# A threshold search over router scores: comparing against base plus step, with the base kept by an accumulator

## What is computed

```python
x = x + xattn(layernorm(x), ctx, ctx, Wq, bq, Wk, bk, Wv, bv)   # softmax(Q K^T / 16) V
# ffn on xt = layernorm(x), 4096 x 256; E = 8 experts, k = 4096 * 2 / 8 = 1024
S = sigmoid(xt @ Wg).T            # 8 x 4096
G, I = top_k(S, k)                # each expert takes its 1024 best rows
ex = xt[I]                        # 8 x 1024 x 256
hid = gelu(ex @ W1 + b1)          # 8 x 1024 x 1024
out = (hid @ W2 + b2) * G
x = x + zeros.at[I].add(out)
```

## Time and profile before

| what | value |
|---|---|
| median of 3 runs | 569.58 us |
| profiled execution | 573.77 us |
| its span | 571.9 us |
| PE busy | 498.6 us (87%) |
| DVE busy | 349.2 us (61%) |
| ACT busy | 303.8 us (53%) |
| POOL busy | 297.3 us (52%) |
| mean granted clock of PE | 0.923 of full speed |

### The profile page before, as it was taken

The page is one execution under the profiler, slowest core; times in us unless marked ns, Lnnn a source line. Parts: engine busy times, 40 slices in busy tenths (PEclk is TensorE's granted clock), DMA queues, the critical chain, the costliest instruction groups (busy, mean ns, idle before and its releaser), DMA issues.

```text
span 571.9 us, 10360 instructions
## 1 busy us (share of the span) xinstructions
PE 498.6 (87%) x3667; PEld 354.5 (62%) x3667; DVE 349.2 (61%) x759; ACT 303.8 (53%) x544; POOL 297.3 (52%) x431
## 2 busy tenths in 40 slices
PE   4599898898633339999999999999999999999995
PEld 4378587676531124586487487487487487487484
DVE  4468888887678863754754753753753853842721
ACT  3556555444723304925934934943943943953931
POOL 2435988797460041673564564474465365366045
PEclk9989899898855556999999999999999999999998
DMA  8952444554351012494484385385385376274024
GB/s 212 309 198 76 107 112 107 146 130 120 93 142 51 0 44 70 131 176 66 132 166 75 119 159 92 111 151 107 108 145 116 101 144 124 85 157 56 0 29 47
DMA packets 92343, 64.57 MB, mean 113 GB/s; under 512 B 53076, under 2 KB 88216, under 8 KB 92312
## 3 DMA queue, kind: packets, MB, share of 16 engines
q1 hardware_dynamic: 79664, 46.82, 30.9%
q0 software_dynamic: 12288, 17.05, 18.3%
q10 hardware_dynamic: 360, 0.30, 0.2%
HBM read 36.22 MB, written 16.91 MB: 93 GB/s over the span
## 4 chain that ended last, share of the span: by engine, by line
PE 59%; POOL 12%; DVE 7%; issue 7%; SPq 6%; DMA 6%; ACT 3%; POOLq 0%; DVEq 0%; ACTq 0%
PE bank L980 54%; SPq L260 6%; POOL xn L366 3%; DMA rows_d<-xrow 3%; PE bank L1185 3%; POOL xrow L359 2%; POOL out L456 2%; DVE junk L754 2%; DMA ctx<-in_ctx 1%; POOL xrow L357 1%; ACT xn L483 1%; DVE kint L787 1%; DMA out<-yo,ids_s 1%; POOL ex L443 1%; PE bank L1118 1%
## 5 line engine op out<-in xcount | busy, mean ns | idle before, releaser
L980 PE MATMUL bank<-w2h,xres 128*128 128x256 f16 x1024 | 169.0, 273 | 0.0
L980 PE MATMUL bank<-exT,w1h 128*128 128x512 f16 x512 | 154.7, 384 | 0.6 <-DVE exT L966 0.6
L980 PE MATMUL bank<-w2l,xres 128*128 128x256 f16 x512 | 139.6, 273 | 0.0
L925 DVE TENSOR_TENSOR xres<-g,xres 128x512 f16<-128x512 f32 x128 | 87.6, 690 | 62.5 <-ACT xres L592 62.5
L456 POOL DMA_INDIRECT out<-yo,ids_s x64 | 101.4, 1584 | 25.8 <-issue 25.2
L980 PEld LDWEIGHTS bank<-w2h,xres 128*128 128x128 f16 x1024 | 100.2, 98 | 12.5
L588 ACT ACTIVATE g<-bank,b1e 128x512 f32<-128x512 f32 x128 | 88.1, 688 | 27.2 <-PE bank L980 22.3
L980 PE MATMUL bank<-exT,w1l 128*128 128x512 f16 x256 | 98.3, 384 | 0.0
L605 ACT ACTIVATE yo<-yt,ge 128x256 f32<-128x256 f32 x64 | 32.6, 509 | 119.5 <-DVE yt L939 119.5
L980 PEld LDWEIGHTS bank<-exT,w1h 128*128 128x128 f16 x512 | 50.2, 99 | 60.4 <-issue 3.0
L592 ACT ACTIVATE xres<-bank,b1e 128x512 f16<-128x512 f32 x128 | 87.3, 682 | 0.0
(11 more groups left out here) (201 smaller groups left out, 813.9 us busy)
## 6 DMA issues: line engine op xcount, KB each, us to landing
w1r<-in_L_ffn_W SPq DMA_DIRECT2D x8, 1024.0 KB, 6.7
w2r<-in_L_ffn_W SPq DMA_DIRECT2D x8, 1024.0 KB, 5.7
ctx<-in_ctx SPq DMA_DIRECT2D x8, 512.0 KB, 5.5
out<-xres SPq DMA_DIRECT2D x8, 512.0 KB, 4.5
rows_d<-xrow SPq DMA_DIRECT2D x8, 512.0 KB, 3.2
xres<-in_x SPq DMA_DIRECT2D x1, 3072.0 KB, 15.7
xres<-in_x SPq DMA_DIRECT2D x2, 512.0 KB, 8.7
b_bc<-in_L_ffn_b SPq DMA_DIRECT2D x8, 128.0 KB, 3.6
```

Source lines behind the costliest of these rows:

```text
L925: dve.tensor_tensor(hid[1][:, f, h * 512:(h + 1) * 512], g32[:, u % 2, :], hid[0][:, f, h * 512:(h + 1) * 512], ALU.subtract).then_inc(s[" ...
L980: last = pe.matmul(out, lhs(a, c), rhs(b, c), start=i == 0, stop=i == len(terms) - 1)
```

## The change

The base of the search is no longer folded into thresholds. A table `gain` holds for each round three copies of the step and, in column 3, the base.

- DVE's two counts become scalar_tensor_tensor instructions: key minus base (a pointer scalar), compared with one or two steps from the table `apart12`, which is broadcast over 256 elements; the accumulator gives the count.
- `passed` becomes (total >= 1024) * gain over four columns. The fourth total is a constant 2048, written once by an extra matmul ahead of round 0, so that the fourth product is the base itself. The accumulator of this instruction is the next base and goes straight to column 3 of the next row of `gain`. L768, L775 and L777 are gone, and `digit_s` with them.
- ACT forms its own candidate ahead of each Sign: an ACTIVATE (Identity) on 128x1 that adds the base to `upto3`. Sign then waits for it, and runs with scale -1.
- POOL's memsets are 62, all at k = 2 (before: 57 at k = 2 and 51 at k = 6).

```diff
-                if k in (2, NP - 2):
-                    pool.memset(sgn[:, 0:4:2] if k == 2 else sgn[:, 1:4:2], 1.0)
+                if k == 2:
                     for r in range(ROUNDS):
-                        if (r < HI_ROUNDS) == (k == 2):
-                            nxt = STEP[r + 1] if r + 1 < ROUNDS else 0.0
-                            pool.memset(move[:, r, 0:2], STEP[r])
-                            pool.memset(move[:, r, 2:3], -STEP[r])
-                            pool.memset(move[:, r, 3:4], STEP[r])
-                            pool.memset(ahead[:, r, 0:1], nxt)
-                            pool.memset(ahead[:, r, 1:2], 2.0 * nxt)
-                            pool.memset(ahead[:, r, 2:3], 0.5 - 3.0 * nxt)
-                            pool.memset(ahead[:, r, 3:4], 0.0)
-                    if k == NP - 2:
-                        pool.memset(c128[:], 128.0).then_inc(s["srch_c"], 1)
+                        pool.memset(gain[:, r + r // HI_ROUNDS, 0:3], STEP[r])
+                        pool.memset(apart12[:, r, 0:1], STEP[r])
+                        pool.memset(apart12[:, r, 1:2], 2.0 * STEP[r])
+                        pool.memset(upto3[:, r:r + 1], 3.0 * STEP[r] - 0.5)
+                    pool.memset(gain[:, 0:HI_ROUNDS + 2:HI_ROUNDS + 1, 3:4], 0.0)
+                    pool.memset(c128[:], 128.0).then_inc(s["srch_c"], 1)
...
             for r in range(ROUNDS):
-                act.wait_ge(s["thr_s"], r + 1)
+                if r:
+                    act.wait_ge(s["thr_s"], r)
+                if r >= 2:
+                    act.wait_ge(s["srch_act"], r - 1)
+                b = r + r // HI_ROUNDS
+                act.activation(thr3[:, r % 2:r % 2 + 1], gain[:, b, 3:4], ACT.Identity, bias=upto3[:, r:r + 1]).then_inc(s["thr3_s"], 1)
...
+                act.wait_ge(s["thr3_s"], r + 1)
...
-                    act.activation(asign[:], khi[:] if r < HI_ROUNDS else krel[:], ACT.Sign, bias=thr[:, 2:3],
+                    act.activation(asign[:], khi[:] if r < HI_ROUNDS else krel[:], ACT.Sign, bias=thr3[:, r % 2:r % 2 + 1], scale=-1.0,
                                    accum_out=cnt[:, 2:3]).then_inc(s["srch_act"], 1)
...
-            def count_pair(keys, r):
+            def search_round(keys, r):
+                b = r + r // HI_ROUNDS
                 for c in range(2):
-                    dve.tensor_scalar(junk[:, c], keys[:], thr[:, c:c + 1], None, ALU.is_ge, ALU.add,
-                                      accum_out=cnt[:, c:c + 1]).then_inc(s["srch_cmp"], 1)
...
-                count_pair(keys, r)
+                    dve.scalar_tensor_tensor(junk[:, c], keys[:], gain[:, b, 3:4], apart12[:, r, c:c + 1].unsqueeze(2).broadcast_to([P, 2, P]),
+                                             ALU.subtract, ALU.is_ge, accum_out=cnt[:, c:c + 1]).then_inc(s["srch_cmp"], 1)
+                dve.wait_ge(s["srch_mm"], r + 1)
+                dve.scalar_tensor_tensor(passed[:], A_[:, 1, 0:4], float(K), gain[:, b, :], ALU.is_ge, ALU.mult,
+                                         accum_out=gain[:, b + 1, 3:4]).then_inc(s["thr_s"], 1)
                 dve.wait_ge(s["thr_s"], r + 1)
-                dve.scalar_tensor_tensor(offs[:], sgn[:], thr[:, 3:4], ahead[:, r, :], ALU.mult, ALU.add).then_inc(s["offs_s"], 1)
-                dve.wait_ge(s["srch_mm"], r + 1)
-                dve.tensor_scalar(passed[:], A_[:, 1, 0:3], float(K), None, ALU.is_ge, ALU.add,
-                                  accum_out=digit[:]).then_inc(s["digit_s"], 1)
-                dve.wait_ge(s["digit_s"], r + 1)
-                dve.wait_ge(s["offs_s"], r + 1)
-                if last is None:
-                    dve.scalar_tensor_tensor(thr[:], move[:, r, :], digit[:, 0:1], offs[:], ALU.mult, ALU.add).then_inc(s["thr_s"], 1)
-                else:
-                    dve.scalar_tensor_tensor(last, move[:, r, 3:4], digit[:, 0:1], offs[:, 3:4], ALU.mult, ALU.add).then_inc(s["t1_s" if r < HI_ROUNDS else "t2_s"], 1)
...
+            pe.matmul(A_[:, 1, 3:4], same16[:], c128[:], start=True, stop=True, skip_group_check=True)
             for r in range(ROUNDS):
                 if r:
-                    pe.wait_ge(s["digit_s"], r)
+                    pe.wait_ge(s["thr_s"], r)
```

More of the change, by code:

```diff
@@ L136, in build @@
         c128 = sb("c128", [P, 1], BF16)
[L137 to L144, removed]
+        passed = sb("passed", [P, 4])
+        gain = sb("gain", [P, ROUNDS + 2, 4])
+        apart12 = sb("apart12", [P, ROUNDS, 2])
+        upto3 = sb("upto3", [P, ROUNDS])
+        thr3 = sb("thr3", [P, 2])
+        t12i = sb("t12i", [P, 2], I32); tshl = sb("tshl", [P, 1], I32); kthi = sb("kthi", [P, 1], I32)
         cnt = sb("cnt", [P, 3], BF16)
@@ L197, in build @@
             x2_tr x2_ev l_mm l_ev
-            gate_r st_gate key_tr key_ev srch_c kint_s khi_s klo_s krel_s krel2_s thr_s offs_s srch_cmp srch_act srch_mm digit_s t1_s t2_s t12i_s tshl_s kth_s half_s
+            gate_r st_gate key_tr key_ev srch_c kint_s khi_s klo_s krel_s krel2_s thr_s thr3_s srch_cmp srch_act srch_mm t12i_s tshl_s kth_s half_s
             kq_s kq_mm above_s tot_s pref_mm pos_a pos_s split_i early_s
@@ L748, in _ @@
             phase_a(body)
-            def count_pair(keys, r):
+            def search_round(keys, r):
+                b = r + r // HI_ROUNDS
                 for c in range(2):
-                    dve.tensor_scalar(junk[:, c], keys[:], thr[:, c:c + 1], None, ALU.is_ge, ALU.add,
-                                      accum_out=cnt[:, c:c + 1]).then_inc(s["srch_cmp"], 1)
[L757 to L764, removed]
-                count_pair(keys, r)
-                dve.wait_ge(s["thr_s"], r + 1)
-                dve.scalar_tensor_tensor(offs[:], sgn[:], thr[:, 3:4], ahead[:, r, :], ALU.mult, ALU.add).then_inc(s["offs_s"], 1)
-                dve.wait_ge(s["srch_mm"], r + 1)
-                dve.tensor_scalar(passed[:], A_[:, 1, 0:3], float(K), None, ALU.is_ge, ALU.add,
-                                  accum_out=digit[:]).then_inc(s["digit_s"], 1)
-                dve.wait_ge(s["digit_s"], r + 1)
-                dve.wait_ge(s["offs_s"], r + 1)
-                if last is None:
-                    dve.scalar_tensor_tensor(thr[:], move[:, r, :], digit[:, 0:1], offs[:], ALU.mult, ALU.add).then_inc(s["thr_s"], 1)
-                else:
-                    dve.scalar_tensor_tensor(last, move[:, r, 3:4], digit[:, 0:1], offs[:, 3:4], ALU.mult, ALU.add).then_inc(s["t1_s" if r < HI_ROUNDS else "t2_s"], 1)
+                    dve.scalar_tensor_tensor(junk[:, c], keys[:], gain[:, b, 3:4], apart12[:, r, c:c + 1].unsqueeze(2).broadcast_to([P, 2, P]),
[3 more added lines that the diff above has]
+                                         accum_out=gain[:, b + 1, 3:4]).then_inc(s["thr_s"], 1)
+                dve.wait_ge(s["thr_s"], r + 1)
             dve.wait_ge(s["srch_c"], 1)
-            dve.memset(sgn[:, 2:3], -1.0)
-            first_thresholds(0)
             dve.wait_ge(s["key_ev"], 1)
@@ L794, in _ @@
                     dve.tensor_copy(klo[:], kint[:, 1]).then_inc(s["klo_s"], 1)
-                if r < HI_ROUNDS - 1:
-                    dve.wait_ge(s["thr_s"], r + 2)
-            dve.wait_ge(s["t1_s"], 1)
-            dve.tensor_scalar(krel[:], khi[:], t12[:, 0:1], float(4 ** HI_ROUNDS), ALU.subtract, ALU.mult).then_inc(s["krel_s"], 1)
-            dve.wait_ge(s["srch_act"], HI_ROUNDS)
-            first_thresholds(HI_ROUNDS)
+            dve.tensor_scalar(krel[:], khi[:], gain[:, HI_ROUNDS, 3:4], float(4 ** HI_ROUNDS), ALU.subtract, ALU.mult).then_inc(s["krel_s"], 1)
             dve.wait_ge(s["krel_s"], 1)
@@ L804, in _ @@
             dve.wait_ge(s["krel2_s"], 1)
-            dve.wait_ge(s["thr_s"], HI_ROUNDS + 1)
             for r in range(HI_ROUNDS, ROUNDS):
-                search_round(krel, r, t12[:, 1:2] if r == ROUNDS - 1 else None)
-                if r < ROUNDS - 1:
-                    dve.wait_ge(s["thr_s"], r + 2)
-            dve.wait_ge(s["t2_s"], 1)
-            dve.tensor_copy(t12i[:], t12[:]).then_inc(s["t12i_s"], 1)
+                search_round(krel, r)
+            dve.tensor_copy(t12i[:], gain[:, HI_ROUNDS:ROUNDS + 2:ROUNDS + 1 - HI_ROUNDS, 3]).then_inc(s["t12i_s"], 1)
             dve.wait_ge(s["t12i_s"], 1)
```

5 lines of the change are left out of this document (2 added, 3 removed).

## The result

| | before | after |
|---|---|---|
| median of 16 runs each | 571.14 us | 565.86 us |
| profiled execution | 573.77 us | 566.57 us |
| mean granted clock of PE | 0.923 | 0.933 |
| one round of the search | 1.63 us | 1.44 us |
| end of the keys' sigmoid to the first `passed` | 8.06 us | 4.65 us |

The ratio is 0.9878 [0.9844 to 0.9913]: 1.2% faster, or 7 us by the ratio and 5.3 by the medians. I had forecast 0.5%, 3.0 us: the sign is right, the size is not. The median itself, 565.86, lies inside the 564.3 to 569.9 of the forecast, but those were counted from 569.58 for the kernel before, and 16 runs put that kernel at 571.14.

The account below looks back on a forecast made before the run. The line 980 matmuls carry the chain, with search and POOL's attention work also on it. Search -1.93, POOL -1.27 and +0.17 make -3.03 us: 570.7 profiled, 566.5 us from the 569.58 median; range 564.3 to 569.9.

Parts of the forecast that it names:

- Round 0 starts late for a reason that the change leaves alone.: Start of the search: DVE's integer operation L787 takes 4.30 us beside a POOL instruction, before and after alike.
- POOL term: Attention stages: 51 memsets gone at k = 6 save 1.27 us; five more at k = 2 cost 0.17 us.
- ACT becomes the later one: Search rounds: with its own candidate ACT needs 1.12 us to L1161, DVE 0.99, so ACT decides by 0.13.
- my 1.52: Search: predicted length of one round in us, 0.11 less than the kernel before.
- The 0.07 for a pair: PE in a search round: one weight load and matmul take 0.07 us, entered as 0.08 from L1159 to L1161.
- the rival of two cycles an element: DVE's counts in each round: 0.53 us more, a round 1.92, the whole slower at 572.9 us; chance 0.12.
- my 1.27: POOL in stage 7: cast of rows 1.27 us earlier without the k = 6 memsets, bounds 0 and 1.75.
- the POOL gain does not come through: Way to the router: only the search gains, 1.9 us less 0.17, giving 567.8 us; chance 0.20.
- the clock's rise in the first expert: PE behind the search: full clock may come earlier or later in the first expert, 0.8 us either way.
- Theory A: Formed after the result: rounds save 2.9 us; the rest is a race ahead of round 0 between masking and iota.
- B: Formed after the result: the rest of the gain is POOL's lighter work at k = 6, carried to the end.
- C: Formed after the result: the rest of the gain is PE's clock, which differs from execution to execution.

Follow-up runs that it names:

- section 3: Experiment on POOL's k = 6 memsets alone: moved to POOL's start in the kernel before (567.4 us), 51 put back in the changed kernel (569.33 us); both repeated with masking late.
- e9: Changed kernel with ACT's candidate formed twice in each round, the second waiting for the first: 573.81 us, ratio 0.9996.
- e2: Kernel before with the constants of k = 6 written at POOL's start, so no memsets at k = 6: 567.4 us, ratio 0.996.
- a4: Changed kernel unchanged, its fourth profiled execution: 565.57 us, 4.60 us to the first `passed`.
- e1: Kernel before with DVE's masking of the low key bits moved from ahead of round 0 into round 5: 567.91 us, ratio 0.9953.
- e7: Changed kernel with 51 memsets put back at k = 6 and the masking moved into round 5: 563.37 us, ratio 0.9873.
- e4: Changed kernel with the masking of the low key bits moved into round 5: 563.34 us, ratio 0.9879 to the kernel before.
- e5: Kernel before with POOL's iota moved to POOL's start, masking left in place: 568.66 us, ratio 0.9948.
- e6: Changed kernel with POOL's iota moved to POOL's start, masking left in place: 563.33 us, ratio 0.9861.
- a2: Changed kernel unchanged, its second profiled execution: 565.23 us, 8.77 us to the first `passed`.

## Why the prediction was wrong

**The step that failed: "Round 0 starts late for a reason that the change leaves alone."** I read the earlier trace rows as a fixed 4.3 us. It is the end of a cascade whose partners start only 0.1 to 0.7 us apart, and my own POOL term moved one of them, as section 3 shows: the work of k = 6 stands ahead of it on POOL's queue. My edit leaves the lines of the cascade alone, but not the times at which they meet. It gave 3.4 us in the profiled pair. Over many executions I put it at some 2.0, as an estimate: the 3.9 us between caught and free in the table (8.33 to 8.77 against 4.60 and 4.65), times the half of the changed kernel's profiles that were free. The means of the profiles, 8.26 us to the first `passed` before (three) and 6.59 after (four), give 1.7. A rival of this kind ("the masking escapes the iota") stood nowhere in my list.

**The rounds: mechanism right, size off.** I had said that ACT becomes the later one, with its candidate at 0.30: measured 0.29 and 0.30, and e9 shows it decides. From T, the end of `passed` (168.49), to L1128 are 1.03, predicted 1.04. The largest miss is that L1130 follows L1128 by 0.04, not 0.08; `passed` to its end takes 0.16, not 0.18, and L1130 to `passed` 0.21, not 0.22. With the 0.01 at L1128 these are the 0.08 by which the round is shorter than my 1.52. Thirteen times 0.19 and twice 0.25 are 2.97; measured 2.90, predicted 1.93. The 0.07 for a pair had been taken from a row of matmuls on 16 columns in a long stream; two small ones that both stand ready start closer.

**The counts: right in the rounds, not ahead of them.** 0.48 each, 0.41 apart; the rival of two cycles an element is refuted. In round 0 of a free execution, though, the first count is held by POOL's subtraction, 2.34 instead of 0.48, where the old form was not. At equal leads the first `passed` comes 1.0 us later than in the kernel before with the masking free (4.65 against 3.63 in e2, leads 0.69 and 0.70) and 1.2 later (a4 4.60 against e1 3.37, leads 0.53). I had put this at nothing. The Trainium skill (Vector Engine (DVE) Microarchitecture Reference, Points that are easy to get wrong) would have had them at half throughput; the rows above decide against it for this form, with 256 float32 keys as one SBUF source, a single float32 number repeated 256 times as the other, and the accumulator. Two sources that are both full rows weren't tried.

**POOL at k = 6: arrived, then given back.** The timelines of `nbias`, the cast of stage 7 and the router after, which answer to the earlier trace rows:
```profile
127.97 1.45 DVE L735 TENSOR_SCALAR nbias<-nmax 128x2 f32<-128x2 f32 x1
...
136.47 1.04 POOL L355 CAST xrow<-xn 128x1024 f16<-128x1024 f32 x1 [0.74 <-POOL xn L364]
...
146.15 0.59 PE L1033 MATMUL bank<-wg,yo 128*128 128x16 f16 x16 [1.93 <-DMA yo<-xrow]
```
`nbias` takes 1.45 instead of 3.56. The cast waits 0.74 for the store, as I had said (the row names POOL's own `xn`, done at 135.72, but the store was issued at 133.11 and lands 3.2 us later), and from the bias add to it are 9.44 us instead of 10.52: 1.08 of my 1.27. But PE now waits 1.93 us for the rows where it had waited 0.24, and its clock stays low for longer. Windows of two us, before and then after (PE, PEld, DVE, ACT, POOL busy, granted clock, DMA share, GB/s):
```profile
148.00:150.00 2.00, 2.00 (x16) 1.64 (x15) 0.81 (x2) 0.25 (x1) 0.00 (x0) 0.77 0.48 155
```
```profile
148.00:150.00 2.00, 2.00 (x12) 1.39 (x10) 0.54 (x2) 0.00 (x0) 0.00 (x0) 0.50 0.61 200
```
From the router to the row transposes behind the 24 matmuls of that stage are 5.22 us instead of 4.32: 0.90 of the 1.08 are lost at 1.2 GHz. The pair e7 and e4 shows the same without the race: 0.6 us lost ahead of the cast with the memsets back (10.20 against 9.58), 0.54 won between the router and the end of the keys' sigmoid (15.29 against 15.83). My rival "the POOL gain does not come through" named this; I had it at 0.20 and my sum took the full term.

**Behind the search.** I allowed 0.8 us either way for the clock's rise in the first expert. Here is more. The windows in which the clock goes to full, before and then after, in the columns just given:
```profile
222.00:226.00 4.00, 4.00 (x16) 1.61 (x14) 1.80 (x4) 2.62 (x5) 0.00 (x0) 0.75 0.35 73
```
```profile
214.00:218.00 4.00, 4.00 (x16) 1.63 (x15) 0.86 (x2) 2.02 (x4) 0.00 (x0) 0.76 0.36 73
```
Expert 0's first matmul starts at 215.23 before and 208.69 after, so the rise lags it by 8.8 and by 7.2 us. Over all profiles the lag has two sizes, 2.5 to 3.7 and 7.2 to 8.8. The short one was met in 8 of 11 profiles of the changed kernel and those made from it and in 1 of 9 of the kernel before and those made from it. From that matmul to the end the profiles of the former take 0.9 us less in the mean (355.3 against 356.2), and this goes with the lag: with the short one it is 354.7 to 355.2, with the long one 356.0 to 356.7, whichever the kernel. Why the changed kernel meets the short one more often wasn't tried.

**The sum by stretches**, from the profiles: us less after than before. First the means of the three profiles of the kernel before and the four of the changed one, then two pairs without the race.

| stretch | before to after | e1 to e4 | e5 to e6 |
|---|---|---|---|
| start to POOL's bias addition of stage 1 | -0.29 | 1.79 | 1.92 |
| from there to the end of the keys' sigmoid | 0.71 | 0.59 | 0.20 |
| to the first `passed` | 1.67 | -1.27 | -0.70 |
| to the keys | 2.93 | 2.92 | 2.94 |
| to expert 0's first matmul | -0.03 | -0.03 | 0.03 |
| to the end | 0.78 | 1.10 | 1.51 |
| span | 5.77 | 5.10 | 5.90 |

Between the two kernels it is the rounds, the race, the clock's rise and up to 0.7 for POOL at k = 6: 5.8 us, between the 5.3 of the medians and the 7.0 of the ratio. Theory A has 4.6 of it, B at most 0.7, C 0.8. With the race gone the price of the held first count shows, and beside the clock's rise 1.8 and 1.9 us of the gain lie in the first 40 us, where the change has no edit. That bias addition starts at 40.6 to 43.0 us in the nine profiles of the kernel before and its variants, and at 38.4 to 43.6 in the eleven of the changed one and its variants, five of them below 40. Why stays open.

## What to carry to other kernels

Where an instruction takes ten times what its group takes elsewhere, it collides with one on another engine: look up which, and how far their starts are apart; if it is less than your change moves, "unchanged" is not an answer, but a case of its own with a price and a chance. Then take the collision away first (here one instruction, moved into a wait, worth 3.2 to 3.8 us in the medians), or each further edit is timed with its luck, as the memsets were here. And an experiment that gives the expected number may give it by another way: only its repetition without the race showed that the memsets by themselves were worth no more than 0 to 0.5 us, less than the medians can tell. Last, look at what a new form of an instruction reads: the counts with two inputs are held by a neighbour that let the old ones through.

## What I had not expected of the hardware

- DVE's shift, conversion and masking of 256 elements (0.28 alone for shift and masking) are kept out for the whole length of a POOL instruction beside them, by an iota that reads nothing as well: 4.30 us beside 4.27. The Trainium skill (SBUF — State Buffer, SBUF: two separate sides) has this as an exclusive lock on a shared port pair, and the trace agrees; it also says that an operation of two SBUF inputs is locked out only by a POOL operation that reads SBUF. The trace agrees there too: the new count took 2.34 beside the subtraction and 0.47 beside the iota, and the old one, with a single such input, 0.48 beside the subtraction. It works the other way round as well: with DVE's shift 0.02 us ahead (e9), POOL's cast took 1.17 instead of 1.04.
- The lock makes chains: released together with the end of one POOL instruction, DVE's next one meets POOL's next. Three instructions of 0.3 to 1 us took 7 us so (162.51 to 169.45 before), and hundredths of a us in a start decided on 4: with the shift 0.03 behind the cast (a2) the masking was caught, with 0.02 ahead of it (e9) it was free.
- A second small matmul whose operands stand ready starts 0.04 us behind the first, with weights of its own.
